# A two-layer decoder block: constants signalled in two parts, GpSimd's bias additions behind the factor tiles, the clock's logarithm second in the second period's chain

## The reference, cut to what matters

```python
x = _layernorm(x + _L0_attn_ref(...)); x = _layernorm(x + _L0_xattn_ref(...)); x = _layernorm(x + _L0_ffn_ref(...))
x = _layernorm(x + _L1_attn_ref(...)); x = _layernorm(x + _L1_xattn_ref(...)); x = _layernorm(x + _L1_ffn_ref(...))

# _L1_attn_ref
xn = _layernorm(x, ln1_g, ln1_b)
q = _l2norm((xn @ Wq).reshape(Bx, Tx, H, Dh)); k = _l2norm((xn @ Wk).reshape(Bx, Tx, H, Dh))
v = (xn @ Wv).reshape(Bx, Tx, H, Dh)
clock = jax.nn.softplus(xn @ clock_w + clock_b)
q = _rope(q, times); k = _rope(k, times)
gj = -jax.nn.softplus(xn @ gate_w + gate_b)
gcp = jnp.exp(jnp.clip(jnp.cumsum(gj, axis=1), -60.0, 50.0))
q = q * gcp; k = k / (gcp + 1e-08)
p = xn @ p_w + p_b
p_exp = jnp.exp(p - jnp.max(p, axis=1)) * clock
p_cs = jnp.cumsum(p_exp, axis=1)
q = q / (p_cs + 1e-08); k = k * p_exp
scores = q k^T / sqrt(Dh), causal; attn = softmax(scores)
x1 = (attn v) @ out_w + out_b + residual
h = _layernorm(x1, ln2_g, ln2_b)
return x1 + gelu(h @ mlp_w1 + mlp_b1) @ mlp_w2 + mlp_b2
```

## Time and profile before

| | |
|---|---|
| median of 3 runs | 1275.82 us (1272.18 to 1276.39) |
| the profiled execution, its own time | 1278.56 us |
| its span in the trace | 1276.8 us |
| busy: TensorE, VectorE, ScalarE, GpSimd | 1121.2, 746.6, 549.3, 460.3 us |
| mean granted TensorE clock | 0.951 of 2.4 GHz |
| chain of waits, largest shares | TensorE 17%, issue 8%, VectorE 8%, ScalarE 3%, GpSimd 3% |

### The profile page before, as it was taken

One profiled execution on the slowest core, in us unless ns is written; L12 is line 12 of the kernel. 1 busy time (PEld: TensorE's weight loads), 2 busy tenths in 40 slices (PEclk: granted clock), 3 DMA queues, 4 the chain that ended last, 5 costly groups with the idle time before them and its releaser, 6 DMA issues. The chain is left out here.

```text
span 1276.8 us, 20429 instructions
## 1 busy us (share of the span) xinstructions
PE 1121.2 (88%) x6750; PEld 795.4 (62%) x6750; DVE 746.6 (58%) x2260; ACT 549.3 (43%) x1411; POOL 460.3 (36%) x539
## 2 busy tenths in 40 slices
PE   7899988998899797799999937689898899999996
PEld 3466455644664476699999924455655575566774
DVE  1473367247634855556555546658739876966356
ACT  1371247125512641233333318356566656734541
POOL 0151025004500684566666641414322612322022
PEclk9999999999999998799999968589999999989999
DMA  6000020020001004661111122100100100000001
GB/s 196 17 1 1 17 57 2 1 56 18 1 1 56 2 22 158 214 193 51 50 44 50 46 91 95 34 1 5 30 8 1 34 9 17 1 1 25 1 1 33
DMA packets 40228, 52.38 MB, mean 41 GB/s; under 512 B 10780, under 2 KB 33372, under 8 KB 40124
## 3 DMA queue, kind: packets, MB, share of 16 engines
q1 hardware_dynamic: 31100, 36.66, 9.0%
q0 software_dynamic: 3408, 9.31, 2.6%
q10 hardware_dynamic: 5616, 5.11, 1.2%
HBM read 41.76 MB, written 9.31 MB: 40 GB/s over the span
## 5 line engine op out<-in xcount | busy, mean ns | idle before, releaser
L1632 PE MATMUL bank<-words 128*128 128x256 f32 (+3 forms) x872 | 273.8, 466 | 13.7 <-DVE words L3049 2.4
L1632 PEld LDWEIGHTS bank<-words 128*128 128x128 f32 (+1 forms) x872 | 166.7, 198 | 94.1 <-issue 59.3
L419 PE MATMUL bank<-words 128*128 128x512 f32 x384 | 171.7, 598 | 8.4 <-DMA words<-in_wq 8.4
L371 POOL TENSOR_TENSOR words<-words 128x256 f32<-128x256 f32 (+1 forms) x128 | 103.6, 832 | 176.6 <-DVE words L972 176.6
L1182 PEld LDWEIGHTS bank<-words 128*128 128x128 f32 x1248 | 147.3, 194 | 3.5 <-ACT words L1216 1.6
L1182 PE MATMUL bank<-words 128*128 128x128 f32 x1248 | 147.8, 277 | 0.9 <-ACT words L1216 0.9
L754 ACT ACTIVATE words<-words 128x128 f32<-128x128 f32 (+1 forms) x256 | 113.3, 444 | 52.7 <-DVE words L967 52.7
L419 PEld LDWEIGHTS bank<-words 128*128 128x128 f32 x384 | 72.1, 192 | 89.7 <-issue 89.2
L706 ACT ACTIVATE words<-bank 128x512 f32<-128x512 f32 x48 | 28.7, 598 | 191.2 <-PE bank L419 191.2
L1231 ACT ACTIVATE words<-words 128x1024 f32 x39 | 41.1, 1057 | 145.2 <-PE bank L1182 113.8
L808 DVE COPY words<-bank 128x512 f32<-128x512 f32 x48 | 33.1, 691 | 104.9 <-PE bank L419 104.6
(11 more groups left out here) (353 smaller groups left out, 2008.1 us busy)
## 6 DMA issues: line engine op xcount, KB each, us to landing
words<-in_w SPq DMA_DIRECT2D x8, 1024.0 KB, 9.3
y_slots<-words ACTq DMA_DIRECT2D x39, 128.0 KB
words<-in_w SPq DMA_DIRECT2D x8, 512.0 KB, 9.9
words<-in_xt SPq DMA_DIRECT2D x4, 512.0 KB, 4.0
words<-in_x SPq DMA_DIRECT2D x4, 512.0 KB, 4.1
x_rows<-words SPq DMA_DIRECT2D x16, 128.0 KB, 1.8
words<-in_wm SPq DMA_DIRECT2D x2, 1024.0 KB, 6.4
out_x<-words SPq DMA_DIRECT2D x16, 128.0 KB, 1.8
```

The lines of the kernel that those rows point to most:

```text
L371: last = pool.tensor_tensor(part, part, inv[:, j % SLOTS0, :, t:t + 1].to_broadcast([P, 2, P * (t + 1)]), ALU.mult)
L419: last = pe.matmul(bank[c % 2][:, :], w, r, start=k == 0, stop=k == KD - 1)
L1632: last = pe.matmul(out, w, r, start=i == 0, stop=i == len(pairs) - 1)
```

## The change

It has three parts.

1. `constants()` raises a new semaphore `biases` behind its first five memsets, before the wait for `n3.normed`. ScalarE waits for `biases` instead of `const` ahead of `first_forms(0)`, and for `const` later, before it first writes `va` (`value_copy`). ScalarE's `front_rows(0, 1)` moves from inside `first_forms(0)` (behind the first two forms) to ahead of that wait. TensorE's and VectorE's waits for `const` stay where they are.
2. GpSimd waits in every period for all four factor tiles of the group (`qkt`) before its two `add_rows`.
3. ScalarE's chain of the second period takes the form of the other periods: the clock's logarithm stands second, the norms' logarithm behind the gate's.

```diff
@@ -1358,7 +1358,7 @@
         lastxr, lastxk, lastrl, lastrs = (cut(gating, 1024 * i, dims) for i, dims in enumerate(((KD, GT), (KD, GT), (KD, GT), (NT, D))))
 
         early, rows = keep["early"], keep["rows"]
-        weights, loaded, const, stored = (sem(f"l_{n}") for n in ("weights", "loaded", "const", "stored"))
+        weights, loaded, const, stored, biases = (sem(f"l_{n}") for n in ("weights", "loaded", "const", "stored", "biases"))
         backed = [sem(f"backed{n}") for n in range(2 * NT)]
         fmm, fmread, qkmm, sqd, vmm, vcop = (sem(n) for n in ("fmm", "fmread", "qkmm", "sqd", "vmm", "vcop"))
         lgate, clr, gcr, ginv, uready, clogged, pmaxed, pexp, sumr, lsum, qsum, qfr, kfr = (sem(n) for n in (
@@ -1502,6 +1502,8 @@
                 pool.memset(mask1[:, :], 3e38)
                 pool.memset(maskx[:, :], 0.0)
                 pool.memset(x5t[:, :, :, 0:1], 0.0)
+                pool.drain()
+                pool.nop().then_inc(biases, 1)
                 pool.wait_ge(n3.normed, NT)
                 pool.memset(va[:, :, :, :], 0.0)
                 pool.drain()
@@ -1544,6 +1546,7 @@
             pool.wait_ge(vmm, NT)
             gather(1)
             pool.wait_ge(n4.normed, NT)
+            pool.wait_ge(qkt, NT)
             add_rows(0, 0, lambda t: x1[:, t, :]).then_inc(biased0, 1)
             add_rows(0, 1, lambda t: x(0, t))
             front_rstd(1, 0)
@@ -1579,6 +1582,7 @@
                     gather(a + 1)
                 if a is not None:
                     pool.wait_ge(n4.normed, NT * a + NT)
+                    pool.wait_ge(qkt, NT * a + NT)
                     add_rows(a, 0, lambda t: x1[:, t, :]).then_inc(biased0, 1)
                     add_rows(a, 1, lambda t: x(a, t))
                     if a + 1 < G:
@@ -2323,8 +2327,6 @@
                 part = batch(b)
                 first_rectified(b, 0, gsum, gabs)
                 first_rectified(b, 1, gsum, gabs)
-                if b == 0:
-                    front_rows(0, 1)
                 first_rectified(b, 2, csum, cabs)
                 act.drain()
                 act.activation(gabs[:, :, part], gabs[:, :, part], ACT.Exp, scale=-1.0)
@@ -2341,6 +2343,7 @@
             def first_rows(b):
 
                 square(0, HALF * b)
+                act.wait_ge(const, 1)
                 value_copy(0, HALF * b)
                 value_copy(0, HALF * b + 1)
                 act.wait_ge(pmaxed, b + 1)
@@ -2371,7 +2374,8 @@
                 act.wait_ge(qsum, b + 1)
                 act.activation(qfac[:, :, part], qfac[:, :, part], ACT.Exp, scale=-1.0).then_inc(qfr, 1)
 
-            act.wait_ge(const, 1)
+            front_rows(0, 1)
+            act.wait_ge(biases, 1)
             first_forms(0)
             front_turned(0, 1)
             first_rows(0)
@@ -2462,7 +2466,7 @@
                     for c in range(4):
                         gelu(r, c)
                     act.preload_act_table_set("natural_log_exp_and_others")
-                if z is not None:
+                if a is not None:
                     act.wait_ge(clr, gates_of(a) + 1)
                     act.activation(gabs[:, :, :], gsum[:, :, :], ACT.Exp, scale=-1.0)
                     act.wait_ge(sumr, gates_of(a) + 1)
@@ -2474,24 +2478,11 @@
                     act.drain()
                     act.activation(gabs[:, :, :], gabs[:, :, :], ACT.Exp, scale=-1.0).then_inc(ginv, 1)
                     act.activation(rn[:, :], rn[:, :], ACT.Exp, scale=-0.5).then_inc(rnr, 1)
-                    for b in range(2):
-                        act.wait_ge(n7.turned, 2 * z + b + 1)
-                        act.activation(x5t[:, :, b, 1:S + 1].rearrange("p k (t n) -> p k t n", t=HALF), turned_rows(bank[6 + b]),
-                                       ACT.Copy).then_inc(n7.copied, 1)
-                    act.wait_ge(qsum, gates_of(a) + 1)
-                    act.activation(qfac[:, :, :], qfac[:, :, :], ACT.Exp, scale=-1.0).then_inc(qfr, 1)
-                elif a is not None:
-                    act.wait_ge(clr, gates_of(a) + 1)
-                    act.activation(gabs[:, :, :], gsum[:, :, :], ACT.Exp, scale=-1.0)
-                    act.wait_ge(ssready, squares_of(a + 1))
-                    act.activation(rn[:, :], ss[:, :], ACT.Ln)
-                    act.drain()
-                    act.activation(gabs[:, :, :], gabs[:, :, :], ACT.Ln, bias=tiny[:, :])
-                    act.activation(rn[:, :], rn[:, :], ACT.Exp, scale=-0.5).then_inc(rnr, 1)
-                    act.drain()
-                    act.activation(gabs[:, :, :], gabs[:, :, :], ACT.Exp, scale=-1.0).then_inc(ginv, 1)
-                    act.wait_ge(sumr, gates_of(a) + 1)
-                    act.activation(qfac[:, :, :], qfac[:, :, :], ACT.Ln, bias=tiny[:, :]).then_inc(lsum, 1)
+                    if z is not None:
+                        for b in range(2):
+                            act.wait_ge(n7.turned, 2 * z + b + 1)
+                            act.activation(x5t[:, :, b, 1:S + 1].rearrange("p k (t n) -> p k t n", t=HALF), turned_rows(bank[6 + b]),
+                                           ACT.Copy).then_inc(n7.copied, 1)
                     act.wait_ge(qsum, gates_of(a) + 1)
                     act.activation(qfac[:, :, :], qfac[:, :, :], ACT.Exp, scale=-1.0).then_inc(qfr, 1)
                 if r is not None or z is not None:
```

## The result

The changed kernel took **1267.80 us** (median of 6 runs, 1264.48 to 1269.05), the kernel before beside it 1275.37 (6 runs, 1272.18 to 1276.39). The ratio is 0.994, 95% interval 0.9921 to 0.9958: 7.6 us less, 5.4 to 10.1 by the interval. The forecast was 1264.1, with a range of 1257.5 to 1270.0. On another chip of the experiments the same change gave 0.9893 (0.9874 to 0.9911), 13.7 us. The interval of the first measurement lies short of the forecast gain of 11.7, and the second holds it.

A forecast was written before the change was run, and what follows sets the result against it. The prediction saw TensorE mostly busy but held by other engines' chains at the start, second period and last full period. Gains 4.6 + 3.1 + 4.05 = 11.75 us took the median 1275.82 to 1264.1; range 1257.5 to 1270.0.

The forecast's parts named there:

- Part 1, 4.6 us: At the start, TensorE goes on without its 4.62 us pause and the whole rest moves 4.6 us earlier; bounds 2.9 to 6.0.
- the working had 2.9: At the start, ScalarE's first form begins at about 763.5 instead of 766.39, 2.9 us earlier.
- Part 3, 3.1 us: Second period: VectorE's norm products start at about 891.4 instead of 894.51, 3.1 us earlier; bounds 2.0 to 3.6.
- so it ends not at 889.4 but at about 890.2: Second period: VectorE's addition meets GpSimd's `add_rest` and takes 2.33 us instead of 1.23.
- Part 2, 4.05 us: Last full period: norm products to first MLP filler take 14.23 us instead of 18.28, gaining 4.05; bounds 3.46 to 5.5.
- I take 0 and keep 1.5: First two periods: about seven `combine` meet an addition, 0.2 us each, 1.5 us at most, mostly covered, so counted as nothing.
- one of the prediction's own signs of being wrong: A `combine` in the first or second period taking 0.6 us or more with scores waiting for it.
- Rival (b): Additions fully block seven `combine` at 0.69 us each, 4.8 us lost uncovered, giving 1268.9; chance 0.08.
- (a): The start's gain is lost again before the second period as the clock pattern shifts, giving 1268.7; chance 0.15.
- (c): Other waits end at the same moment, so only the start's gain counts, giving 1271.2; chance 0.07.
- (d): Slower: the thinner start leaves TensorE at 1.2 GHz from 776 to 806, costing 18.4 us, giving 1282.5; chance 0.03.
- The unexplained wait of 3.56 us: A wait before a factor tile that the trace lays to no engine; the high-end sum let it go by the shift.

The follow-up runs named there:

- e1: Kernel before with only the constants raised in two parts and ScalarE's second pair of rows moved ahead; 1276.95 us, ratio 0.9968.
- e2: Kernel before with only the new order of ScalarE's chain in the second period; 1277.45 us, ratio 0.9977 to the kernel before.
- e12: Kernel before with the constants in two parts and both GpSimd waits, without ScalarE's new order; 1269.91 us, ratio 0.9917.
- after: The changed kernel with all three parts, as profiled with the first measurement; median 1267.80 us, profiled execution 1269.05 us.
- e7: The changed kernel with no edit, run again on another chip; 1267.53 us, ratio 0.9893 to the kernel before.
- e10: The changed kernel without both GpSimd waits on the factor tiles; 1272.76 us, ratio 0.9944 to the kernel before.
- e11: Kernel before with GpSimd's wait on the factor tiles added in the last full period only; 1272.57 us, ratio 0.9949.
- e3: Kernel before with only GpSimd's two waits on the factor tiles, covering all periods; 1273.88 us, ratio 0.9942.
- e9: The kernel before with no edit, run again on a chip of the experiments; 1278.62 us, ratio 0.9997.
- e8: Second run of the changed kernel with GpSimd's new wait kept only in the last full period; 1266.39 us, ratio 0.9887.
- e5: Changed kernel with GpSimd's additions moved behind the next block's norm root in the first two periods; 1265.93 us, ratio 0.9883 to the kernel before.
- e6: Changed kernel with a drain behind each of GpSimd's eight additions, in every period; 1266.13 us, ratio 0.9889 to the kernel before.
- e4: Changed kernel with GpSimd's new wait kept only in the last full period; 1266.58 us, ratio 0.9888 to the kernel before.

## Why the prediction came out as it did

The three parts did what the forecast said of them, and its range held the time. The gain on the first chip, 7.6 us, fell short of the 11.75 by more than its interval allows, and on the experiments' chip it was 13.7, with one term too small. By its own steps:

**Part 1, 4.6 us.** In e1 the third form came 5.1 us earlier, the first factor tile 5.3 and the first mask 4.6 (53.7 to 49.1), and 4.1 were left in the time. In the changed kernel the first form came 2.8 us earlier, where the working had 2.9. The third form came 5.6 earlier, at the high side, with a granted clock of 0.82 in 762 to 776 instead of 0.62. It was 5.8 at the first factor tile.

**Part 3, 3.1 us.** The time says 2.9 alone (e2) and 3.1 on top of e12, as forecast. One term inside was mis-sized: the step "so it ends not at 889.4 but at about 890.2" took 2.33 us for an addition that meets GpSimd, and it took 2.86 in after, e7 and e2 and 2.87 in e10, since it met all of `add_rest`. From the chain alone e10 against e1 gives 2.3 us. The rest of the 3.1 cannot be laid to a single row: behind the products the distance to the second period's fifth mask is 15.5 us in e10 and 16.6 in e1, at a granted clock of 1.00 and 0.90. But before has 15.1 at 0.89, so the clock alone does not explain it, and it stays open.

**Part 2, 4.05 us.** This is the term that failed by size on the experiments' chips: 6.5 (e11) and 7.4 us (e3). VectorE's part was right, 4.19 and 2.73 us for products and mixes, 3.5 us less up to the first factor tile. Missing were two things. What is left at the first mask varies with the clock that the stretch had without the wait: 2.1 us where it was 0.90 (e11 against e9), 4.7 where it was 0.73 (e12 against e10), instead of one fixed 4.05. And the working had no term for the 1.5 to 1.7 us near the end. Together they are 3.8 us for e11 against e9, whose traces differ by 5.6 and whose times by 6.5: another 1.8 lie ahead of the fourth period (370.3 and 368.5), where both kernels are the same. So the 6.5 is not fully accounted for.

**"I take 0 and keep 1.5" for `combine`.** The working expected seven short collisions of 0.2 us each. What came in after was one long block in each of the first two periods, 3.75 and 3.05 us, with scores waiting behind the first, which is one of the prediction's own signs of being wrong. In that trace the gather's end and not the new wait released the additions, and VectorE arrived earlier than in before; in e7's first period the wait did release them. By the medians of e7 against e8, e5 and e6 the blocking costs 1.1 to 1.6 us, so the bound of 1.5 roughly held, but for another reason than the one given, and with luck: other executions of the same kernel had no block of over 3 us. The rule of the Trainium skill, page "SBUF — State Buffer", section "Who interferes with whom", an exclusive lock between an instruction of VectorE with two SBUF inputs and one of GpSimd that reads SBUF, fits the rows in kind, and the price put on it, up to 0.69 for each of seven, did not: a single `combine` was held for 3.75. Rival (b), a full block that costs 4.8 us, is not borne out by e8, e5 and e6.

**Rivals (a), (c), (d).** The start's gain was not lost again: e10 has 7.2 us where e2 alone has 2.9. All three parts count. The granted clock did not fall in 776 to 790 (1.00) and was 0.79 in 790 to 806 against 0.81. A shift can bring another pattern there, as (a) says: in e1, e10, e12 and e4 the stretch as far behind the gather had 0.68, and their first mask came at 49.1 to 49.2 and not at 47.7 to 48.1. Since e4 and e8 (49.2 and 47.8) are the same kernel, such a difference of 1.4 us between two traces says nothing on an edit.

**The unexplained wait of 3.56 us** The earlier trace rows is not the change's to take away. It shrank to 0.74 in after, but the same kernel in e7 has 3.60. Timeline of VectorE in after, then in e7:

```profile
814.87 0.42 DVE L2679 TENSOR_TENSOR words<-bank,words 128x256 f32<-128x256 f32 x1 [0.74 <-PE bank L1836]
```

```profile
816.16 0.42 DVE L2679 TENSOR_TENSOR words<-bank,words 128x256 f32<-128x256 f32 x1 [3.60 <-remote]
```

In e5 and e11 it is 2.86 and 2.83, laid to TensorE as in after. The factor tile behind it came 8.6 us earlier in after than in before (75.5 to 66.9 us behind the gather) and 6.0 in e7. At the first period's 13th mask, behind the blocked `combine`, both had 5.8 left (87.3 to 81.6 and 81.5).

**The first measurement.** 7.6 us against 13.7 on another chip. The changed kernel took 1267.8 and 1267.5 us on the two; it is the kernel before that took 1275.4 on one and 1279.8 to 1281.0 on the others. No part was measured alone on the first chip, so which term fell short there is not known. The trace of before from one of the others (e9) has 532.8 us from gather to end, against 531.3; the expectation of 534 or more was wrong, and the 5 us are not found. One reason is that the profiled execution of before took 1278.56, above all of the timed runs beside it, so no trace shows one of its short runs. What makes this kernel shorter on the first chip stays open. The two profiled executions differ by 12.0 us behind the gather, where the sum of the working was 11.75.

## What to carry to other kernels

When the engine that feeds TensorE gets faster, look at two prices: the engine's own time, and the granted clock of the stretch behind it. Here the engine's own 3.5 us were worth 2.1 at the first mask where the clock had been 0.90, and 4.7 where it had been 0.73. A moved instruction meets its neighbours in new places, and the collision to look for is the one of whatever arrives earlier, not only of what was moved. Align two traces at the first instruction that the change can reach before comparing them, and take a second execution of the same kernel before explaining a row by the edit: the longest blocked `combine` and the short wait of 0.74 us stood in one trace of the changed kernel and not in the other. Compare parts by their ratios to the kernel before, run beside them: so taken the parts added, while the gain of the whole differed by 6 us between chips.

## What the runs showed of the hardware

A row of GpSimd additions without gaps (eight of 0.71 us, one every 0.68) can hold a VectorE instruction with two SBUF inputs until the row ends: 3.75 us over five additions and 3.05 over four in after, 2.01 over the last three in e7. It does not always: two `combine` inside one row in e7, and likewise in e3 and e12, got through after one addition each (0.84 and 1.03 us), and in the fourth period of the kernel before the two engines took turns for 9 us, 1.2 us an instruction on both sides. With a drain between the additions (e6) none took longer than 0.8 us in the first period. Which of the two patterns comes was not settled; in the two long blocks of after the `combine` started within 0.02 us of an addition.

Near the end TensorE pauses for 2.21 us and then again, for 2.2 to 2.4 us, in all the traces. The granted clock dropped behind one of the two in all five traces without GpSimd's last wait (behind the first in four, behind the second in before) and behind neither in the nine with it, though the last instructions that differ lie over 120 us ahead.
